# The product with the values placed between the scores of the two tiles of an attention step

## The chip, the cores and the metric

The kernel runs on one core of one Trainium2 chip. The metric is the time of one execution on the device, in microseconds (us); lower is better.

## The reference

Four layers run one after the other over 1024 tokens (4 sequences of 256) of width 512, each with a layer norm ahead of it and a residual behind it: a state-space layer, a sparse feed-forward layer, a latent attention layer, and a clustered feed-forward layer. The change touches the third:

```python
q_c = hidden_size @ Wq_c.T + bq_c
q = (q_c @ Wq_up.T + bq_up).reshape(b, s, NH, Q_HEAD).transpose(0, 2, 1, 3)   # 32 heads, 192 wide
kv = hidden_size @ Wkv_c.T + bkv_c                                            # 64 latent + 64 rope
kvu = (kv_nope @ Wkv_up.T + bkv_up).reshape(b, s, NH, QK_NOPE + V_HEAD)...
scores = jnp.einsum('bhqd,bhkd->bhqk', q, k) / np.sqrt(Q_HEAD)
attn = jax.nn.softmax(scores, axis=-1)
o = jnp.einsum('bhqk,bhkv->bhqv', attn, v)
out = jnp.einsum('bhsv,Hv->bsH', o, Wo) + bo
```

The output projection is the same for every head, so the sum over the heads is formed first. Keys and values are used in their latent form: per head the key weights are folded into the query weights.

## The kernel before

Every engine has its own program, written out by hand, and the engines meet at counting semaphores: `wait_ge` on one side, `then_inc` on the other. What stands in an engine's program runs in that order.

The attention works in tiles numbered `w` from 0 to 127. A tile is one head of one sequence: its 256 queries (two blocks of 128) by 256 keys. `w` counts through 16 head pairs `i`, in each through 4 sequences, in each through the two heads of the pair. The loop of line 1138 takes two tiles in one step, `w` and `w+1`, with `v = w mod 8`, so one pair has four steps: v = 0, 2, 4 and 6. This text calls a step by its `w` or its `v`. On TensorE (PE) a step holds

- `scores(w)` and `scores(w + 1)` (L1054, matmuls L1067 to L1069): 6 matmuls of 128x256 each, since the operands are split into a high and a low part. They write bank `C + w % 2`, so `scores(w)` waits until the exponentials of tile `w - 2` have read that bank (`p_e`);
- in one step of a pair also `fold` (L1011, matmuls L1018) or `fold_bias` (L1027, L1031), which make the folded query weights of the pair after next: for pairs 1 to 13 in the steps v = 2 and v = 4. They stand inside `values`;
- `values` (L1084, matmuls L1100): the product of the probabilities of tiles `w - 4` and `w - 3` with the latent values, into 64-column halves of bank B. It waits for the copied probabilities (`pT`) of tile `w - 3`, and for bank B to be read (`oT`, `oT_l`);
- `turn_p` (L1072, L1080): the transposes of the probabilities of tiles `w - 2` and `w - 1`, which wait for the normalised probabilities (`p_n`);
- `query` (L1034, L1048 to L1052): 5 matmuls of 128x512 for a pair to come, and in the steps v = 0 and v = 4 `sum_up` (L1104, L1108 to L1110), 3 matmuls.

VectorE (DVE) takes one tile after the other (L2066): the row maxima of tile `w` (`top`, L2048 and L2049), then the normalisation of tile `w - 1` (`norm`, L2053 and L2054), and after every second tile the low part of the values' product (L2044) or of a query (L2035). ScalarE (ACT) does in a step (L1627): the exponentials of `w` (`exp`, L1592), what `fold` left (L1560, L1563, L1571), the values' product (`value`, L1608), the copy of the transposes of `w - 2` (L1601), the exponentials of `w + 1`, the copy of the transposes of `w - 1` (L1601 again), and a query (L1584). That last copy of a step is what `values` of the next step waits for: in step `w`, the copy of tile `w - 3`.

Of the kernel before, what the change touches and what calls it, by code (L numbers as in the profile page):

```python
# [37 lines left out]
NV = 2 * NB * NPAIR  # L38
# [5 lines left out]
A, B, C, E, Y0, Y1, T, S = range(8)  # L44
# [20 lines left out]
def bass_layers(nc, d, out):  # L65
    with ExitStack() as ctx:
# [184 lines left out]
        def fold_step(i):  # L251
            return 2 if i else 4
# [8 lines left out]
        def col(n):  # L261
            return slice(n * P, (n + 1) * P)
# [308 lines left out]
        def _(pe):  # L571
# [3 lines left out]
            def busy(n, bank):  # L575

                for _ in range(n):
                    mm(PS[:, bank, 3 * P:], filler[:, 0:P], filler[:, 0:P], start=True, stop=True)  # L578
# [417 lines left out]
            def latent_B(h, bank):  # L996
                for k in range(KD):
                    for n in range(2):
                        last = mm(PS[n * QB:(n + 1) * QB, bank], w_qc[:, k, P:QL], xn[:, k, half(h)], start=(k == 0), stop=(k == KD - 1))
                last.then_inc(s["qc_ps"], 1)  # L1000

            def latent_kv(h, bank):
                project(bank, w_kvc, h).then_inc(s["qc_ps"], 1)

            def keys_turned():
                pe.wait_ge(s["qc"], 6)
                for u in range(NU):
                    last = nc.tensor.transpose(PS[:, S, u * KVL:(u + 1) * KVL], kv[0:KVL, col(u)], identF[0:KVL, 0:KVL])
                last.then_inc(s["qc_ps"], 1)

            def fold(i):  # L1011
                if i:
                    pe.wait_ge(s["cb"], i)
                    pe.wait_ge(s["qb"], i)
                pe.wait_ge(s[f"w_h{i % 2}"], 80 * (i // 2) + 80)
                w = w_h[:, i % 2]
                for n in range(4):
                    last = mm(PS[:, B, SEQ + n * KVL:SEQ + (n + 1) * KVL], w[:, n // 2, col(n % 2)], w[:, n // 2, 2 * P + 1:],  # L1018
                              start=True, stop=True)
                if i < 2:  # L1020
                    fold_bias(i, 0)
                if i == 0:
                    pe.wait_ge(s["a_in"], 16 * 11)
                    mm(PS[KVL:, B, KVL:KVL + NH], bias_rows, identF[0:NH, 0:NH], start=True, stop=True).then_inc(s["qb_ps"], 1)
                last.then_inc(s["cb_ps"], 1)

            def fold_bias(i, at):  # L1027

                w = w_h[:, i % 2]
                for hh in range(2):  # L1030
                    last = mm(PS[0:KVL, B, at + hh:at + hh + 1], w[:, hh, 2 * P + 1:], w[:, hh, 2 * P:2 * P + 1], start=True, stop=True)  # L1031
                last.then_inc(s["qb_ps"], 1)

            def query(i, j):  # L1034
                h, hh = divmod(j, 2)
                pe.wait_ge(s["cb_l"], 2 * i + 2)
                if i == 0 and j == 2:
                    pe.wait_ge(s["ql"], 1)
                elif i == 1 and j == 0:
                    pe.wait_ge(s["ql"], 3)  # L1040
                elif query_bank(i, j) == A and j + i:
                    pe.wait_ge(s["ql"], 4 * i + j)
                R = slice(0, QB)
                a, b, k = 2 * hh, 2 * hh + 1, i % 2
                to = PS[:, query_bank(i, j)]
                if i == 0:
                    pe.wait_ge(s["qc_l"], 3 * h + 2)
                mm(to, lABh[:, k, a], qcAh[:, half(h)], start=True, stop=False)  # L1048
                mm(to, lABh[:, k, a], qcAl[:, half(h)], start=False, stop=False)
                mm(to, lABl[:, k, a], qcAh[:, half(h)], start=False, stop=False)  # L1050
                mm(to, lABh[:, k, b], qcBh[:, half(h)], start=False, stop=False)
                mm(to, lABh[:, k, b], qcBl[:, half(h)], start=False, stop=True).then_inc(s["q_ps"], 1)  # L1052

            def scores(w):  # L1054
                i, v = divmod(w, 2 * NB)
                b, hh = divmod(v, 2)
                pe.wait_ge(s["ql"], 4 * i + b // 2 * 2 + hh + 1)
                if w >= 2:
                    pe.wait_ge(s["p_e"], w - 1)
                elif w == 0:  # L1060
                    pe.wait_ge(s["qc_l"], 3)
                    pe.wait_ge(s["ql"], 2)
                if w == 2 * NB // 2:
                    pe.wait_ge(s["qc_l"], 6)
                for q in range(2):
                    to, c, keys = PS[:, C + w % 2, q * SEQ:(q + 1) * SEQ], col(2 * b + q), slice(b * SEQ, (b + 1) * SEQ)
                    mm(to, qh[i % 2][:, hh, c], kvh[:, keys], start=True, stop=False)  # L1067
                    mm(to, qh[i % 2][:, hh, c], kvl[:, keys], start=False, stop=False)
                    last = mm(to, ql[i % 2][:, hh, c], kvh[:, keys], start=False, stop=True)  # L1069
                last.then_inc(s["s_ps"], 1)  # L1070
# [13 lines left out]
            def values(g, i, v):  # L1084
                b = g % NB
                if g:
                    pe.wait_ge(s["oT"], g)
                    pe.wait_ge(s["oT_l"], g)
                if v == fold_step(i) and i + 2 < NPAIR:
                    fold(i + 2)  # L1090
                elif v == fold_step(i) + 2 and i + 2 < NPAIR:
                    pe.wait_ge(s["cb"], i + 3)
                    fold_bias(i + 2, SEQ)
                else:
                    pe.wait_ge(s["cb"], min(i + 3, NPAIR) if v > 2 else min(i + 2, NPAIR))
                pe.wait_ge(s["pT"], 2 * g + 2)
                pe.wait_ge(s["qc"], 7)
                for kt in range(2):
                    for hh in range(2):
                        last = mm(PS[hh * KVL:(hh + 1) * KVL, B, 0:SEQ], kvT[:, 2 * b + kt], pT[:, (2 * g + hh) % 4, kt],  # L1100
                                  start=(kt == 0), stop=(kt == 1))
                last.then_inc(s["pv_ps"], 1)

            def sum_up(i, h):  # L1104
                k = i % 2
                pe.wait_ge(s["wvl"], i + 1)
                pe.wait_ge(s["oT_l"], NB * i + 2 * h + 2)
                mm(PS[:, Y0 + h], wvh[:, k], oTh[:, half(h)], start=(i == 0), stop=False)  # L1108
                mm(PS[:, Y0 + h], wvl[:, k], oTh[:, half(h)], start=False, stop=False)
                mm(PS[:, Y0 + h], wvh[:, k], oTl[:, half(h)], start=False, stop=(i == NPAIR - 1)).then_inc(s["wv_ps"], 1)  # L1110

            def project_out(h):
                pe.wait_ge(s["bvs"], h + 1)
                if h:
                    pe.wait_ge(s["x3"], KD)
                else:
                    pe.wait_ge(s["pT"], NV - 1)
                for m in range(KD):
                    mm(PS[:, WO_TO[h][m]], w_oT[:, col(m)], osum[:, half(h)], start=True, stop=True).then_inc(s["wo_ps"], 1)  # L1119
# [18 lines left out]
            for w in range(0, NV + 6, 2):  # L1138
                i, v = divmod(w, 2 * NB)
                if w < NV:  # L1140
                    scores(w)
                    scores(w + 1)
                if w == 0:
                    latent_B(1, Y1)
                    latent_kv(1, S)
                if w == 2:
                    keys_turned()
                if NV <= w < NV + 4:
                    busy(20, A)
                if 4 <= w < NV + 4:  # L1150
                    values(w // 2 - 2, i, v)
                if w == NV + 2:
                    busy(24, A)
                    project_out(0)
                if v in (0, 4) and w >= NV:
                    sum_up(i - 1, v // 4)
                if w == 2:
                    query(0, 2)
                    query(0, 3)
                for u in (w, w + 1):  # L1160
                    if 2 <= u < NV + 2:
                        turn_p(u - 2)
                for u in (w, w + 1):
                    if u in QUERY_AT and w > 2:
                        query(*QUERY_AT[u])
                if v in (0, 4) and 2 * NB <= w < NV:
                    sum_up(i - 1, v // 4)
# [1047 lines left out]
```

## Time and profile before

| | |
|---|---|
| median of 3 runs | 2104.95 us (2104.36 to 2105.88) |
| the profiled execution | 2105.0 us, span 2103.2 us |
| TensorE busy | 2066.0 us, 98% |
| VectorE busy | 1603.2 us, 76% |
| ScalarE busy | 1461.1 us, 69% |
| GpSimd busy | 783.9 us, 37% |
| granted TensorE clock | 0.997 of full speed |

Busy time is the union of the records of an engine. The attention loop runs from about 1697 to 2046 us of the span. In rows of the timeline below the first column is the start in us from the span's start, the second the duration in us, then the engine, the line, the operation, its output and input, the shapes and the count; what stands in brackets is idle time of the engine just before, and what ended it.

### The profile page before, as it was taken

How to read it: one execution, taken by the hardware profiler on the slowest of the kernel's cores; microseconds unless marked ns; L12 is line 12 of the kernel's file. 1: busy time of each engine (PE TensorE's matmuls, PEld its weight loads, DVE VectorE, ACT ScalarE, POOL GpSimd, SP SyncE). 2: the span in 40 equal slices, each digit the busy share in tenths (PEclk: the TensorE clock that was granted, in tenths of full speed). 3: DMA queues.
4: the chain of work that ended last, by engine and by line, in shares of the span. 5: the costliest groups of instructions: out<-in, count | busy, mean ns of one | idle time of the engine just before them, and what ended most of it. 6: DMA issues, size and time to landing. Idle time of an engine off the chain costs nothing. (4 is left out here: it accounts for less than half of the span.)

```text
span 2103.2 us, 35260 instructions
## 1 busy us (share of the span) xinstructions
PE 2066.0 (98%) x13530; PEld 1691.3 (80%) x13532; DVE 1603.2 (76%) x1802; ACT 1461.1 (69%) x3188; POOL 783.9 (37%) x433
## 2 busy tenths in 40 slices
PE   8899999999999999999999999999899999999998
PEld 7788888888888888888888888887688768888876
DVE  7778788887877877888788788778653367878775
ACT  4777776777677777677677767775553267787772
POOL 2344444544345444454444543454444300101011
PEclk9999999999999999999999999999999999999999
DMA  3322222222122222222212222122133210101001
GB/s 114 114 81 74 97 101 80 81 101 81 71 101 90 71 101 90 79 92 96 87 71 101 91 71 100 71 99 55 54 98 110 66 46 21 31 21 32 13 2 41
DMA packets 56246, 157.53 MB, mean 75 GB/s; under 512 B 16656, under 2 KB 27152, under 8 KB 47632
## 3 DMA queue, kind: packets, MB, share of 16 engines
q1 hardware_dynamic: 56080, 155.28, 21.4%
q8 instruction: 109, 1.79, 0.3%
q14 instruction: 57, 0.47, 0.1%
HBM read 152.64 MB, written 2.62 MB: 74 GB/s over the span
## 5 line engine op out<-in xcount | busy, mean ns | idle before, releaser
L651 PE MATMUL PS<-xnh,wh 128*128 128x512 f32 x1272 | 510.3, 401 | 3.2 <-DVE arena L1785 1.8
L653 PE MATMUL PS<-xnh,wl 128*128 128x512 f32 x1272 | 496.7, 390 | 0.0
L652 PE MATMUL PS<-xnl,wh 128*128 128x512 f32 x1272 | 495.6, 390 | 0.0
L1779 DVE SCALAR_TENSOR_TENSOR arena<-PS,arena 128x1020 f32<-128x1020 f32 (+2 forms) x240 | 305.6, 1274 | 31.1 <-ACT arena L1328 25.4
L1289 ACT ACTIVATE PS<-x,arena 128x128 f32<-128x128 f32 x1024 | 309.4, 358 | 20.7 <-DVE arena L1811 19.7
L461 POOL TENSOR_TENSOR zl<-arena,zh 128x1024 fp32r<-128x1024 f32 x63 | 176.6, 2803 | 293.7 <-ACT zh L1311 293.7
L651 PEld LDWEIGHTS PS<-xnh,wh 128*128 128x128 f32 x1272 | 238.8, 188 | 57.7 <-issue 8.2
L653 PEld LDWEIGHTS PS<-xnh,wl 128*128 128x128 f32 x1272 | 238.7, 188 | 51.9
L652 PEld LDWEIGHTS PS<-xnl,wh 128*128 128x128 f32 x1272 | 239.3, 188 | 45.7
L457 POOL TENSOR_TENSOR arena<-arena 128x1024 f32<-128x1024 f32 x63 | 151.8, 2409 | 298.0 <-ACT arena L1307 298.0
L446 POOL TENSOR_TENSOR wl<-arena,wh 128x1024 fp32r<-128x1024 f32 x72 | 174.6, 2425 | 198.7 <-ACT wh L1278 198.7
L651 PE MATMUL PS<-zh,woh 128*128 128x512 f32 x496 | 194.2, 392 | 1.4 <-DVE arena L1809 1.4
L653 PE MATMUL PS<-zh,wol 128*128 128x512 f32 x496 | 194.1, 391 | 0.0
L652 PE MATMUL PS<-zl,woh 128*128 128x512 f32 x496 | 193.8, 391 | 0.0
L1817 DVE TENSOR_TENSOR sq<-sq,PS 128x1024 f32<-128x1024 f32 x124 | 150.7, 1221 | 42.9 <-PE PS L653 42.8
L1802 DVE TENSOR_TENSOR arena<-PS,arena 128x1024 f32<-128x1024 f32 x64 | 78.4, 1225 | 130.3 <-PE PS L686 130.3
L710 PE MATMUL PS<-arena 128*64 128x128 f32 x2048 | 171.0, 277 | 4.0 <-DVE arena L1811 4.0
L1324 ACT ACTIVATE arena<-PS 128x1024 f32<-128x1024 f32 x64 | 65.8, 1028 | 147.8 <-PE PS L653 147.8
L1809 DVE TENSOR_TENSOR arena<-PS,arena 128x1024 f32<-128x1024 f32 x128 | 156.1, 1220 | 3.8 <-ACT PS L1293 1.6
L1300 ACT ACTIVATE PS<-x,arena 128x128 f32<-128x128 f32 x512 | 154.5, 360 | 1.5 <-DVE arena L1809 1.5
L1592 ACT ACTIVATE arena<-PS,arena 128x256 f32<-128x256 f32 x256 | 119.4, 474 | 50.7 <-DVE arena L2049 50.4
L710 PEld LDWEIGHTS PS<-arena 128*64 128x64 f32 x2048 | 120.7, 138 | 26.6 <-issue 26.6
(283 smaller groups left out, 4222.6 us busy)
## 6 DMA issues: line engine op xcount, KB each, us to landing
x<-decay SPq DMA_DIRECT2D x64, 1024.0 KB, 4.6
arena<-in_w_xg SPq DMA_DIRECT2D x72, 512.0 KB, 5.4
arena<-in_w_o SPq DMA_DIRECT2D x32, 512.0 KB, 3.5
arena<-in_w_f SPq DMA_DIRECT2D x28, 512.0 KB, 3.5
x<-in_x SPq DMA_DIRECT2D x3, 1024.0 KB, 6.6
arena<-in_w_h SPq DMA_DIRECT2D x16, 192.0 KB, 2.9
arena<-in_w_h SPq DMA_DIRECT2D x16, 129.0 KB, 2.8
out<-x SPq DMA_DIRECT2D x8, 256.0 KB, 2.0
```

The costliest lines, as they stand in the source:

```text
L446: nc.gpsimd.tensor_tensor(wl[:, k], w_raw, wh[:, k].bitcast(F32), ALU.subtract).then_inc(s["wlo"], 1)
L457: nc.gpsimd.tensor_tensor(sumsq, sumsq, ysq, ALU.add).then_inc(s["ssq"], 1)
L461: nc.gpsimd.tensor_tensor(zl[:, k], zt[:, k], zh[:, k].bitcast(F32), ALU.subtract).then_inc(s["zlo"], 1)
L651: mm(PS[:, bank], ah, bh, start=(n == 0), stop=False)
L652: mm(PS[:, bank], ah, bl, start=False, stop=False)
L653: last = mm(PS[:, bank], al, bh, start=False, stop=(n == len(terms) - 1))
L710: last = mm(PS[H, YB + u // 4, col(u % 4)], xdt[:, u, H], ring[:, hh, col(u)], start=(u % 2 == 0), stop=True)
L1289: last = act(PS[:, bank + u // 4, col(u % 4)], rowB[:, 2 * k + hh, col(u)], ACT.Relu, scale=-1.0, bias=aT[:, u, 2 * t + hh:2 * t + hh + 1])
L1300: last = act(PS[:, LB + b // 2, col(2 * hh + b % 2)], rowB[:, 2 * k + hh, col(2 * b + 1)], ACT.Exp, bias=fromend[:, k, b, hh:hh + 1])
L1779: ins = stt(o, pair_of(bank).rearrange("p q (b t) -> p q b t", t=SEQ)[:, :, :, :SEQ - k], w[:, 3 - k:4 - k], o, ALU.mult, ALU.add)
L1809: tt(both(ring[:, hh]), pair_of(bank), both(by[:, 0:TOK]), ALU.mult).then_inc(s["used"], 1)
L1817: tt(both(sq[:, m]), both(sq[:, m]), pair_of(bank), ALU.add).then_inc(s["oacc"], 1)
```

## The change

In the loop over the steps, `values` is written between `scores(w)` and `scores(w + 1)` instead of behind both; what `values` contains (`fold` and `fold_bias` among it) moves with it. Behind the last scores, where a step has none, the order stays as it was. Nothing is added or removed, and the programs of the other engines are untouched.

```diff
                 i, v = divmod(w, 2 * NB)
                 if w < NV:
                     scores(w)
+                elif w < NV + 4:
+                    busy(20, A)
+                if 4 <= w < NV + 4:
+                    values(w // 2 - 2, i, v)
+                if w < NV:
                     scores(w + 1)
                 if w == 0:
                     latent_B(1, Y1)
                     latent_kv(1, S)
                 if w == 2:
                     keys_turned()
-                if NV <= w < NV + 4:
-                    busy(20, A)
-                if 4 <= w < NV + 4:
-                    values(w // 2 - 2, i, v)
                 if w == NV + 2:
                     busy(24, A)
                     project_out(0)
```

TensorE's program in a step v = 6 (`w = 70`), before: from the last matmul of the first tile's scores to the transposes. In brackets stand the semaphores that an instruction waits for.

```order
L1069 MATMUL PS<-xnh,wl 128x256
L1067 MATMUL PS<-xnh,wh 128x256 [waits s_p_e,s_ql]
L1068 MATMUL PS<-xnl,wh 128x256
L1069 MATMUL PS<-xnh,wl 128x256
L1067 MATMUL PS<-xnh,wh 128x256
L1068 MATMUL PS<-xnl,wh 128x256
L1069 MATMUL PS<-xnh,wl 128x256
L1100 MATMUL PS<-arena 64x256 [waits s_pT,s_cb,s_qc,s_oT_l,s_oT]
L1100 MATMUL PS<-arena 64x256 x3
L1080 MATMUL PS<-cst,arena 128x128 [waits s_pT,s_p_n]
L1080 MATMUL PS<-cst,arena 128x128 x3
```

The same stretch now:

```order
L1069 MATMUL PS<-xnh,wl 128x256
L1100 MATMUL PS<-arena 64x256 [waits s_pT,s_cb,s_qc,s_oT_l,s_oT]
L1100 MATMUL PS<-arena 64x256 x3
L1067 MATMUL PS<-xnh,wh 128x256 [waits s_p_e,s_ql]
L1068 MATMUL PS<-xnl,wh 128x256
L1069 MATMUL PS<-xnh,wl 128x256
L1067 MATMUL PS<-xnh,wh 128x256
L1068 MATMUL PS<-xnl,wh 128x256
L1069 MATMUL PS<-xnh,wl 128x256
L1080 MATMUL PS<-cst,arena 128x128 [waits s_pT,s_p_n]
L1080 MATMUL PS<-cst,arena 128x128 x3
```

The four matmuls of `values`, with their five waits, have moved ahead of the six of the second tile's scores; the transposes stay where they were. The steps v = 0 have the same rows.

TensorE's program in a step v = 4 of a pair with a fold (`w = 76`), now: from the last matmul of the first tile's scores.

```order
L1069 MATMUL PS<-xnh,wl 128x256
L1031 MATMUL PS<-arena 64x1 [waits s_cb,s_oT_l,s_oT]
L1031 MATMUL PS<-arena 64x1
L1100 MATMUL PS<-arena 64x256 [waits s_qc,s_pT]
L1100 MATMUL PS<-arena 64x256 x3
L1067 MATMUL PS<-xnh,wh 128x256 [waits s_p_e,s_ql]
L1068 MATMUL PS<-xnl,wh 128x256
L1069 MATMUL PS<-xnh,wl 128x256
L1067 MATMUL PS<-xnh,wh 128x256
L1068 MATMUL PS<-xnl,wh 128x256
L1069 MATMUL PS<-xnh,wl 128x256
```

Before, the last six of these rows stood ahead of the first L1031.

## Rows read from the trace of the kernel before

**Rows 1.** Windows view, one head pair: busy us and records by engine, clock, DMA

```profile
1889.90:1911.14 21.24, 21.22 (x152) 17.47 (x150) 17.01 (x40) 16.91 (x53) 2.23 (x3) 1.00 0.10 26
```

**Rows 2.** Timeline of PE, step w = 72 (v = 0)

```profile
1894.55 0.28 PE L1067 MATMUL PS<-xnh,wh 128*128 128x256 f32 x1
...
1895.87 0.28 PE L1069 MATMUL PS<-xnh,wl 128*128 128x256 f32 x1
1896.08 1.09 PE L1100 MATMUL PS<-arena 128*64 128x256 f32 x8
1897.10 1.09 PE L1080 MATMUL PS<-cst,arena 128*128 128x128 f32 x8
...
1899.88 0.28 PE L1067 MATMUL PS<-xnh,wh 128*128 128x256 f32 x1
```

**Rows 3.** Timeline of PE, step w = 76 (v = 4)

```profile
1905.35 0.28 PE L1067 MATMUL PS<-xnh,wh 128*128 128x256 f32 x1
...
1905.94 0.28 PE L1069 MATMUL PS<-xnh,wl 128*128 128x256 f32 x1
1906.24 0.35 PE L1067 MATMUL PS<-xnh,wh 128*128 128x256 f32 x1
1906.44 0.28 PE L1068 MATMUL PS<-xnl,wh 128*128 128x256 f32 x1
```

**Rows 4.** Timeline of ACT, at the same place

```profile
1905.53 0.49 ACT L1592 ACTIVATE arena<-PS,arena 128x256 f32<-128x256 f32 x1
1905.88 0.22 ACT L1592 ACTIVATION_READ_ACCUMULATOR arena<-PS,arena 128x1 f32 x1
1905.97 0.62 ACT L1601 ACTIVATE arena<-PS 128x512 f32<-128x512 f32 x1
```

**Rows 5.** Line L1067: idle time of its engine (us, times) by what ended it

```profile
  issue: 4.1, 16
```

**Rows 6.** Timeline of DVE and ACT, end of step w = 70 (v = 6)

```profile
1893.09 0.68 DVE L2048 TENSOR_REDUCE arena<-PS 128x2 f32<-128x512 f32 x1
1894.01 0.48 ACT L1592 ACTIVATE arena<-PS,arena 128x256 f32<-128x256 f32 x1 [0.27 <-DVE arena L2049]
1894.93 0.59 ACT L1601 ACTIVATE arena<-PS 128x512 f32<-128x512 f32 x1
```

**Rows 7.** Timeline of ACT and PE behind the last scores: copy, then values

```profile
2039.47 0.61 ACT L1601 ACTIVATE arena<-PS 128x512 f32<-128x512 f32 x1
2040.33 1.09 PE L1100 MATMUL PS<-arena 128*64 128x256 f32 x8 [0.74 <-ACT arena L1601]
```

**Rows 8.** Timeline of PE and ACT, step w = 120, last of its kind

```profile
2020.65 0.28 PE L1067 MATMUL PS<-xnh,wh 128*128 128x256 f32 x1
2021.04 0.60 ACT L1601 ACTIVATE arena<-PS 128x512 f32<-128x512 f32 x1
```

**Rows 9.** Timeline of PE, ACT and DVE, fold step w = 74 (v = 2)

```profile
1900.80 0.69 DVE L2048 TENSOR_REDUCE arena<-PS 128x2 f32<-128x512 f32 x1 [1.05 <-PE PS L1069]
1902.25 1.09 PE L1100 MATMUL PS<-arena 128*64 128x256 f32 x8
1903.07 0.68 DVE L2048 TENSOR_REDUCE arena<-PS 128x2 f32<-128x512 f32 x1
1903.38 0.38 ACT L1560 ACTIVATE arena<-PS 128x256 f32<-128x256 f32 x1 [0.63 <-PE PS L1100]
1904.60 0.59 ACT L1601 ACTIVATE arena<-PS 128x512 f32<-128x512 f32 x1
```

**Rows 10.** Timeline of PE and ACT, step w = 124

```profile
2030.05 0.28 PE L1069 MATMUL PS<-xnh,wl 128*128 128x256 f32 x1
2031.25 0.36 PE L1067 MATMUL PS<-xnh,wh 128*128 128x256 f32 x1 [0.92 <-ACT arena L1592]
2032.13 1.09 PE L1100 MATMUL PS<-arena 128*64 128x256 f32 x8
2031.00 0.60 ACT L1601 ACTIVATE arena<-PS 128x512 f32<-128x512 f32 x1
```

## The prediction

> **What bounds the kernel now.** The change touches the attention loop alone, so I read that stretch. The windows view of one head pair comes first: in 21.24 us TensorE is busy 21.22, VectorE 17.01, ScalarE 16.91 [rows 1], at full granted clock. The loop is bound by TensorE, and only two things can move its time: idle time in TensorE's queue, and extra cost where one kind of matmul follows another. The busy share cannot show a short wait, because the record of a scores matmul lasts 0.28 us while the next one starts 0.12 us later (1905.35 to 1905.94 are five such distances [rows 3]). So I read distances between starts, in the timeline.
>
> Nearly every distance is regular. The six matmuls of one tile's scores take 6 x 0.12 = 0.72 us, from the last scores to the values it is 0.21, from the values to the transposes 1.02 [rows 2]. One exception recurs. In step v = 4 of a pair the second tile's scores start 0.30 us after the matmul before them and the next follows after 0.20, where 0.12 is normal: 0.18 + 0.08 = 0.26 us lost [rows 3]. ScalarE shows why: the exponentials of tile w-1, which read the same bank, end at 1905.88 + 0.22 = 1906.10, and the scores start 0.14 us later [rows 4]. It happens in pairs 1 to 13, the ones whose fold delays ScalarE; the summary of line L1067 has 4.1 us of such idle time in 16 places [rows 5], which includes a few at the loop's ends. A second exception is step w = 124, where the second scores start 1.20 us after the matmul before them, again for the exponentials [rows 10]. Almost nothing else on TensorE is waiting, so there is little to gain: 13 x 0.26 = 3.4 us, and about 1.1 us in w = 124.
>
> The Trainium skill (Perfetto Trace Analysis, section Tensor Engine Instruction) says that the end of a matmul in the profile is an estimate from its size. By busy time alone, 0.02 us idle in a pair, the gain would be 13 x 0.02 = 0.3 us in place of 3.4; the starts are recorded, and I go by them.
>
> **The change part by part.** No instruction is added or removed, no DMA moves. 62 steps (w = 4 to 126) have both scores and values and change their order. Each part is the change in TensorE's time, which in a TensorE-bound loop is the change of the kernel.
>
> *The wait that goes.* In step v = 4 about 1.2 us of work (the fold's bias and the values) now lies ahead of the second scores. They come 0.72 + 1.2 = 1.9 us after 1905.35 [rows 3], long after 1906.10. Gain 13 x 0.26 = 3.4 us.
>
> *The wait that comes.* The values need the copied probabilities of tile w-3, which is the last copy ScalarE makes in the step before. In step w = 72 that copy ends at 1894.93 + 0.59 = 1895.52, 0.97 us after the step's first scores at 1894.55 [rows 2, 6]. The values used to start 1.53 us after them (1896.08), now they would after 1.53 - 0.72 = 0.81. So the copy is late. How long after it the values can start is shown behind the last scores, where TensorE stands idle for exactly this: copy ends 2039.47 + 0.61 = 2040.08, values start 2040.33, 0.25 us later [rows 7]. The values then start at 0.97 + 0.25 = 1.22, a stall of 0.41 us. TensorE works in order, so the second scores and all behind them stand still too.
>
> Can the copy come earlier? It follows the exponentials of tile w-1, which start when VectorE has their maxima: 1893.09 to 1894.01, with ScalarE idle for 0.27 us just before [rows 6]. VectorE in turn is full from the first scores of step v = 6 on, taking a tile each 2.3 us, and that start is not moved relative to its step. So the copy stays where it is relative to TensorE, and earlier values do not help it. The stall should appear wherever the step before is a short one, 4.65 us as from 1889.90 to 1894.55 [rows 1, 2]: the 15 steps v = 0 (w = 8 to 120, where the last has the copy's end at 2021.04 + 0.60 = 2021.64, 0.99 us after the scores at 2020.65 [rows 8]), and w = 116, whose step before has no fold. Behind longer steps, with a sum or a fold, the copy ends at 0.3 us or before the scores: no stall.
>
> *The fold steps.* Three things shift in step v = 2. The values come 0.72 us earlier, so ScalarE's 0.63 us wait for them goes [rows 9] and its chain runs ahead. The values start at 1902.25 - 0.72 = 1901.53, the second scores at 1902.55, and the row maxima 0.92 us behind them (1899.88 to 1900.80 for the first tile [rows 2, 9]), at about 1903.5 in place of 1903.07. The exponentials follow another 0.92 later [rows 6], at 1904.4, unless the copy ahead of them holds them: it starts at 1904.60 now [rows 9] and about 0.55 sooner then, since the transposes stay where they are and let it come no earlier. So exponentials and last copy move up 0.5 to 0.6 us, and that copy ends near 1906.59 - 0.6 = 1906.0 [rows 4], 0.65 us after the first scores of step v = 4. With 0.25 added that is 0.90, just ahead of the values there at about 1.0. I cost this at nothing. The cover is thin: if it is gone, step v = 4 has the 0.41 stall too.
>
> *The order of matmul kinds.* The values are 64 columns wide, all around them 128. A step had scores, values, transposes; it now has scores, values, scores, transposes. The number of width changes is the same. New is that scores restart behind the values. When scores restart after a pause, the first takes 0.20 us to the next where 0.12 is normal [rows 3]: 0.08. The transposes no longer restart after the values and give back up to that much. Ends: nothing and 0.08 us a step. I take 0.03, nearer the low end because one restart replaces another: 62 x 0.03 = 1.9 us. In the 16 steps with a stall, that 0.03 of the step before shortens the stall to 0.38: 16 x 0.38 = 6.1 us.
>
> The Trainium skill (TensorEngine Tiling (Array Packing), section Key Properties) says that changing the tiling mode drains TensorE. By that rule alone, both orders have two such changes in a step and this term is zero; the whole sum would be 1.9 us lower. No row here has values followed by scores, so the row of the restart decides.
>
> *The end of the loop.* Without queries the steps are short and TensorE is ahead of ScalarE. In w = 124 the copy that the values need ends at 2031.00 + 0.60 = 2031.60; the values start at 2031.85 (before: 2032.13) and the second scores 1.02 later at 2032.87 (before: 2031.25) [rows 10]. The transposes follow about 0.5 us later than now. In w = 126 the same repeats, with the last scores some 2 us and the last tile's exponentials some 0.9 us later than now; nothing behind them takes up the delay. Cost 0.9 us, ends 0 and 1.5.
>
> Sum: -3.4 + 6.1 + 1.9 + 0.9 = +5.5 us. The profiled execution took 2105.0 us, the median of the runs is 2104.95, so the two hardly differ: 2105.0 + 5.5 = 2110.5 us.
>
> **The rivals.**
> *The new wait is cheap.* The 0.25 us from copy to values is measured on an engine that had stood idle; with 0.6 us of scores running it may partly hide, and the copy may shift. With 0.15 in place of 0.38: -3.4 + 2.4 + 1.9 + 0.5 = +1.4, 2106.4 us, within the noise. For it: only 0.97 against 0.81 is bare lateness. Against: the stretch from copy to values is passing on a signal, which running scores don't shorten.
>
> *Faster.* ScalarE's last copy of a step moves up. If it ends less than 0.81 - 0.25 = 0.56 us after the first scores everywhere, no values wait, the 3.4 us come in whole, and the 1.2 us hole of w = 124 is filled: 2105.0 - 3.4 - 1.2 = 2100.4 us. For it: ScalarE loses the wait for the values in the fold steps. Against: in step v = 6 it waits for VectorE, not for TensorE [rows 6], and that end must come 0.4 us sooner.
>
> *Slower than forecast.* The fold steps' second scores come so late that VectorE and ScalarE carry the delay into step v = 4: values there stall 0.38 us as well, in 13 pairs. 5.5 + 13 x 0.38 = +10.4, 2115.4 us. It decides at a copy that ends later than 0.75 us after the first scores of step v = 4, against my 0.65.
>
> That the change doesn't do what it says can be ruled out: the program's order shows the rows moved.
>
> **How the numbers follow.** About 0.2% (4.2 us) is what a measurement of this kernel can tell from no change. Chances: forecast 0.53, cheap wait 0.25, slower than forecast 0.14, faster 0.08. The forecast's own ends, from a restart at nothing (-1.9, tail -0.9) to one at 0.08 (+3.1), are 2107.7 and 2113.6; a quarter of it lies below 2109.2 and counts as no change. The cheap wait is almost wholly within 0.2%. So slower 0.55, same 0.37, faster 0.08. The range takes in the forecast, the cheap wait with a free restart (2104.5) and nearly all of the slower case: 2104 to 2115.
>
> **What would show each step right or wrong.** In the profile after: the copy still ends 0.97 us after the first scores in steps v = 0, values start 1.22 after them, and TensorE is idle there; a pair takes 21.24 - 0.26 + 0.38 + 0.12 = 21.48 us. In step v = 4 the second scores wait for nothing. ScalarE's wait for the values in fold steps is gone. The distance from a first score behind the values to the next is near 0.20, and from the last scores to the transposes 0.12. The forecast is wrong if values in steps v = 0 start before 1.0, if steps v = 2, 4 or 6 show a wait of the values, or if a pair takes 21.24 us or less.

## The result and the profile after

The changed kernel takes 2110.77 us (median of 8 runs, 2109.33 to 2111.98), the kernel before 2104.51 us beside it (8 runs, 2102.06 to 2107.66). The ratio is 1.0033 with a 95% interval of 1.0023 to 1.0042: slower by 6.3 us, where 5.5 us and a time of 2110.5 us had been forecast.

Single executions of one kernel differ by up to some 3 us from the median, and much of that arises ahead of the attention: in the traces of this study its first matmul (L999) starts anywhere between 1679.2 and 1683.5 us. So the traces are compared by two lengths that leave this out. One is a head pair, from the first scores of w = 70 to those of w = 78. The other is the attention stretch, from the first matmul of `latent_B` (L999) to the first of the output projection (L1119). The summaries of these two lines in the trace of the changed kernel (durations in ns, then first and last start in us):

```profile
L999 PE MATMUL PS<-arena x32: 592/592/643, 1680.2 to 1699.5; 128*64 128x512 f32 x32
```

```profile
L1119 PE MATMUL PS<-arena x16: 591/592/697, 2051.3 to 2060.9; 128*128 128x512 f32 x16
```

The stretch is 371.13 us by the timeline's hundredths. In the kernel before it was 364.55 (1682.42 to 2046.97). The whole difference of 6.58 us is there; what lies behind it takes 56.25 us in both.

The windows view of the changed kernel, the same head pair as in [rows 1] (columns as there: length; busy us and records of PE, weight loads, VectorE, ScalarE, GpSimd; granted clock, DMA share, GB/s):

```profile
1889.39:1910.90 21.51, 21.20 (x152) 17.65 (x150) 17.08 (x40) 16.82 (x54) 2.23 (x3) 1.00 0.10 25
```

21.51 against 21.24 us: the pair is 0.27 us longer, and TensorE's busy time has not grown. The time went into waits. The timeline of TensorE in step w = 72 (v = 0), which answers to [rows 2]:

```profile
1894.06 0.28 PE L1067 MATMUL PS<-xnh,wh 128*128 128x256 f32 x1
...
1894.66 0.28 PE L1069 MATMUL PS<-xnh,wl 128*128 128x256 f32 x1
1895.25 1.09 PE L1100 MATMUL PS<-arena 128*64 128x256 f32 x8 [0.31 <-ACT arena L1602]
1896.26 0.39 PE L1067 MATMUL PS<-xnh,wh 128*128 128x256 f32 x1
1896.49 0.28 PE L1068 MATMUL PS<-xnl,wh 128*128 128x256 f32 x1
...
1896.96 0.28 PE L1069 MATMUL PS<-xnh,wl 128*128 128x256 f32 x1
1897.09 1.03 PE L1080 MATMUL PS<-cst,arena 128*128 128x128 f32 x8
...
1899.81 0.28 PE L1067 MATMUL PS<-xnh,wh 128*128 128x256 f32 x1
```

And ScalarE's copy that it waited for:

```profile
1894.40 0.60 ACT L1602 ACTIVATE arena<-PS 128x512 f32<-128x512 f32 x1
```

The copy ends at 1895.00, 0.94 us after the first scores, and the values start 0.25 us behind it, 1.19 us after those scores instead of the 0.80 us that they take in steps without a wait. The step is 5.75 us long (before: 5.33). The view of waits from 1715 to 2040 us (who waited for whom: us, times, longest) has it as a line of its own, which the kernel before did not have in this window:

```profile
PE PS L1100 <- ACT arena L1602: 6.7, 17, 1.5
```

The 17 places are 14 of the steps v = 0 and the steps w = 116, 124 and 126. The fifteenth step v = 0, w = 8, is not among them: its copy ends at 0.71 and its values start at 0.96, so it loses only 0.16 us to the wait.

Steps v = 4 of the pairs with a fold have lost their wait. TensorE in step w = 76, which answers to [rows 3]:

```profile
1905.31 0.28 PE L1067 MATMUL PS<-xnh,wh 128*128 128x256 f32 x1
...
1905.91 0.28 PE L1069 MATMUL PS<-xnh,wl 128*128 128x256 f32 x1
1906.12 0.34 PE L1031 MATMUL PS<-arena 128*64 128x1 f32 x3
...
1907.36 0.38 PE L1067 MATMUL PS<-xnh,wh 128*128 128x256 f32 x1
1907.58 0.28 PE L1068 MATMUL PS<-xnl,wh 128*128 128x256 f32 x1
```

Everything follows at the normal distances. The step takes 5.58 us (before: 5.79). Its copy, on ScalarE:

```profile
1905.33 0.60 ACT L1602 ACTIVATE arena<-PS 128x512 f32<-128x512 f32 x1
```

It ends 0.62 us after the first scores, and the values start normally at 0.95. Steps v = 2 with a fold take 5.50 us (before 5.47), steps v = 6 take 4.67 (before 4.65). So a pair changes by +0.41 - 0.21 + 0.03 + 0.02 = +0.25, and 0.27 in the windows.

Added up over the loop, step by step: 14 steps v = 0 at +0.415 and w = 8 at +0.18 make +6.0; w = 116 +0.4; 13 steps v = 4 -2.7; 13 steps v = 2 +0.4; 13 steps v = 6 +0.3; w = 6, which had a wait of its own, -0.2; the other steps up to w = 122 +0.2; w = 124 +0.4; and from the first scores of w = 126 to the output projection +1.7 (13.94 against 12.20). That is +6.5. The last item was not foreseen in this size. VectorE there, between the last scores and the last values but one, in the changed kernel:

```profile
2041.45 1.02 DVE L2050 TENSOR_SCALAR arena<-arena 128x2 f32<-128x2 f32 x1
2042.39 0.15 DVE L2054 RECIPROCAL arena<-arena 128x2 f32<-128x2 f32 x1
2042.57 1.64 DVE L2055 TENSOR_TENSOR arena<-arena 128x512 f32<-128x512 f32 x1
2044.14 0.41 DVE L2045 TENSOR_TENSOR xnl<-PS,xnh 128x256 fp32r<-128x256 f32 x1
2044.47 0.15 DVE L2054 RECIPROCAL arena<-arena 128x2 f32<-128x2 f32 x1
2044.66 1.24 DVE L2055 TENSOR_TENSOR arena<-arena 128x512 f32<-128x512 f32 x1
```

These operations elsewhere take 0.17 (L2050) and 0.69 us (L2055). At the same time GpSimd works on the next layer's weights, and TensorE waits for VectorE's low part:

```profile
2041.19 5.85 POOL L560 TENSOR_TENSOR zl<-arena,zh 128x512 fp32r<-128x512 f32 x4
```

```profile
2044.65 1.09 PE L1100 MATMUL PS<-arena 128*64 128x256 f32 x8 [1.98 <-DVE xnl L2045]
```

### The profile page after: what moved, and what is told of

Its sections match the earlier page's. It is cut to its first block, busy times and chain, and to the rows that moved or that the text cites. A ratio compares the mean times of both kernels' runs of the same rounds, so it can differ in the third digit from the quotient of the medians.

```text
span 2107.6 us, 35262 instructions
## 1 busy us (share of the span) xinstructions
PE 2064.1 (98%) x13532; PEld 1692.6 (80%) x13532; DVE 1605.1 (76%) x1802; ACT 1457.3 (69%) x3188; POOL 784.2 (37%) x433
## 4 chain that ended last, share of the span: by engine, by line
PE 87%; DVE 7%; ACT 2%; issue 1%; DMA 1%; SPq 1%; POOL 0%; ACTq 0%; DVEq 0%
PE PS L651 19%; PE PS L653 19%; PE PS L652 19%; PE PS L710 6%; PE PS L919 3%; PE PS L686 3%; PE PS L706 3%; PE PS L1100 2%; PE PS L1080 2%; PE PS L1067 1%; DVE arena L2049 1%; PE PS L1069 1%; PE PS L1068 1%; DVE arena L1780 1%; PE PS L644 1%
```

## The experiments

Two theories stood against each other. **The waits**: the change costs where the values wait for ScalarE's copy, in the steps behind a short step and at the loop's end, and gains where the scores no longer wait for the exponentials. **The restart**: scores behind values cost some 0.10 us in each of the 62 steps. Both give the 6.6 us, but at different places. Runs 1, 2, 3 and 5 choose the order step by step. They use this form of the loop, each with a condition of its own (the edit is against the changed kernel):

```diff
+                between = 4 <= w < NV and (CONDITION)
                 if w < NV:
                     scores(w)
                 elif w < NV + 4:
                     busy(20, A)
-                if 4 <= w < NV + 4:
+                if between:
                     values(w // 2 - 2, i, v)
                 if w < NV:
                     scores(w + 1)
+                if 4 <= w < NV + 4 and not between:
+                    values(w // 2 - 2, i, v)
```

| kernel | attention stretch, us | against before | time, us (ratio to before, 95%) |
|---|---|---|---|
| before | 364.55 | | |
| the change | 371.13 | +6.58 | 2110.77 (1.0033, 1.0023 to 1.0042) |
| 1: v = 4 alone | 364.70 | +0.15 | 2104.83 (1.0005, 0.9997 to 1.0014) |
| 2: v = 0 alone | 370.98 | +6.43 | 2110.01 (1.0030, 1.0019 to 1.0040) |
| 3: old order in w = 124, 126 | 368.75 | +4.20 | 2108.61 (1.0023, 1.0015 to 1.0032) |
| 4: change, GpSimd late | 369.87 | +5.32 | 2108.46 (1.0023, 1.0014 to 1.0032) |
| 5: v = 2 and v = 4 | 362.13 | -2.42 | 2101.42 (0.9988, 0.9979 to 0.9997) |
| 6: change, copy's wait first | 368.95 | +4.40 | 2109.31 (1.0023, 1.0014 to 1.0032) |
| 7: change, slower copy | 377.08 | +12.53 | 2115.26 (one execution) |
| 8: before, slower copy | 364.49 | -0.06 | 2106.02 (one execution) |
| 9: before, GpSimd late | 364.57 | +0.02 | 2102.11 (one execution) |
| 10: as 5, GpSimd late | 361.99 | -2.56 | 2099.4 (one execution) |

**1. The new order in the fold steps v = 4 alone** (CONDITION: `v == 4 and i + 2 < NPAIR`). The condition takes in w = 4 of the first pair too, so 14 steps change.

> The values go between the scores only in the 13 steps v = 4 whose pair folds; the other 49 steps keep the order of before. Theory of the waits (what the change costs hangs on where it is made): these steps lose their wait for the exponentials and are 0.20 us shorter each, no values wait for a copy; 13 x 0.20 = 2.6 us faster than before, a head pair takes 21.24 - 0.20 = 21.04 us. Theory of the restart (scores behind values cost some 0.10 us in each place, 6.6 us over 62 steps): 13 x 0.10 = 1.3 us slower than before.

Nothing came: the stretch is 0.15 us longer, and the 13 fold steps take 5.82 or 5.83 us, 0.04 more than before and not the 5.58 expected. Step w = 6 behind w = 4 is 0.24 us shorter, which takes back about half of that. This falls under neither theory as I had put it. The timeline of TensorE and ScalarE in step w = 76, whose first scores start at 1904.66:

```profile
1905.25 0.28 PE L1069 MATMUL PS<-xnh,wl 128*128 128x256 f32 x1
1905.46 0.39 PE L1031 MATMUL PS<-arena 128*64 128x1 f32 x4
1905.95 1.09 PE L1100 MATMUL PS<-arena 128*64 128x256 f32 x8
```

```profile
1905.28 0.62 ACT L1605 ACTIVATE arena<-PS 128x512 f32<-128x512 f32 x1
```

The copy ends at 1905.90, 1.24 us after the first scores as in the kernel before, and the values wait for it in place of the scores. In the changed kernel it ends at 0.62, because there the values of step v = 2 are moved as well and let ScalarE's `fold` start sooner; run 5, which moves both, has it at 0.62 again. The gain of one step hangs on the order of the step before. The run gave one more thing: here the values start 0.05 us behind the copy, not 0.25.

**2. The new order in the 15 steps v = 0 alone** (CONDITION: `v == 0`).

> The values go between the scores only in the 15 steps v = 0. Theory of the waits: the values wait for the copy there and each step is 0.41 us longer (the first of them 0.2): 15 steps make 5.9 us over before, nearly the whole of the loss, a head pair takes 21.24 + 0.41 = 21.65 us, and no step v = 4 gains. Theory of the restart: 15 x 0.10 = 1.5 us over before.

The stretch is 6.43 us longer, the 15 steps take 5.76 to 5.78 us and the pair 21.67:

```profile
1890.16:1911.83 21.67, 21.30 (x152) 17.57 (x150) 17.09 (x40) 16.80 (x53) 2.22 (x3) 1.00 0.11 26
```

15 of 62 places carry almost the whole loss. The restart theory, which gave 1.5 us, falls.

**3. The old order in the last two steps** (CONDITION: `w < NV - 4`).

> As the change, but the steps w = 124 and 126 keep the order of before. Theory of the waits: the last two steps and what follows them cost 2.2 us in the changed kernel (0.44 in step 124, 1.73 behind the first scores of step 126), and with the old order there this goes: 6.6 - 2.2 = 4.4 us over before. Theory of the restart: 60 of the 62 places are left, 6.4 us over before.

+4.20 us against 4.4 expected: the end of the loop is worth 2.4 us, with 12.19 us from the first scores of w = 126 to the output projection, as before.

**4. GpSimd's next work held back.**

```diff
+            po.wait_ge(s["p_n"], NV)
             for k in range(KD):
                 po.wait_ge(s["wd_h"], k + 1)
```

> The changed kernel, with GpSimd's four subtractions for the next layer's weights (L560) waiting for the last normalisation. Theory of the collision (those 5.9 us of GpSimd work slow VectorE's last tiles: L2050 took 1.02 instead of 0.17 us, L2055 1.64 and 1.24 instead of 0.69): these durations return to normal and the kernel is 1.5 to 2 us faster than the changed one, some 4.8 us over before. If the two only happen at the same time, the durations stay and the time is that of the changed kernel.

VectorE's durations returned to normal, where the changed kernel had 1.02 and 1.64:

```profile
2040.58 0.17 DVE L2051 TENSOR_SCALAR arena<-arena 128x2 f32<-128x2 f32 x1
2040.65 0.16 DVE L2055 RECIPROCAL arena<-arena 128x2 f32<-128x2 f32 x1
2040.84 0.69 DVE L2056 TENSOR_TENSOR arena<-arena 128x512 f32<-128x512 f32 x1
```

So the subtractions do slow them. The gain in the stretch is 1.26 us, a little under the 1.5 to 2 us expected: once VectorE is on time, ScalarE's copy is the next wait.

**5. The new order in the steps v = 2 and v = 4 of pairs 1 to 13** (CONDITION: `v in (2, 4) and 0 < i and i + 2 < NPAIR`).

> The values go between the scores in the steps v = 2 and v = 4 of the 13 pairs 1 to 13, and nowhere else. The first run with v = 4 alone kept ScalarE's late copy (1.24 us after the first scores), because the values of step v = 2 were not moved. Theory of the waits, mended: with both moved the copy of step v = 2 ends 0.6 us after the first scores of step v = 4 as in the changed kernel, steps v = 4 take 5.58 us (before 5.79) and steps v = 2 take 5.50 (before 5.47), the others stay: a pair takes 21.24 - 0.17 = 21.07 us, 2.3 us less over the loop. Theory of the restart: 26 restarts and no wait gone, 2.6 us more.

All of it came. The steps take 5.58 (v = 4) and 5.50 us (v = 2), the others keep their lengths, the stretch is 2.42 us shorter than before, and the pair:

```profile
1886.29:1907.36 21.07, 21.07 (x152) 17.51 (x150) 17.02 (x40) 16.89 (x54) 2.23 (x3) 1.00 0.11 27
```

By the distances between starts, no step of this pair has a wait left on TensorE. The time is 2101.42 us against 2104.43 beside it, ratio 0.9988 with an interval that ends below 1. This version is faster than both kernels.

**6. The copy's wait written first.** In steps without a fold:

```diff
+                plain = i + 2 >= NPAIR or v not in (fold_step(i), fold_step(i) + 2)
+                if plain:
+                    pe.wait_ge(s["pT"], 2 * g + 2)
                 if g:
                     pe.wait_ge(s["oT"], g)
...
-                pe.wait_ge(s["pT"], 2 * g + 2)
+                if not plain:
+                    pe.wait_ge(s["pT"], 2 * g + 2)
```

> The changed kernel, with the wait for the copied probabilities written first of the five waits of the values, so that it is the one taken last in front of the matmul. Theory of the queued waits (0.20 of the 0.25 us from copy to values are the other waits, taken one after the other behind it; in the run with v = 4 alone, where that wait stood alone with one other, the values started 0.05 us behind the copy): in steps v = 0 the values start 1.00 us after the first scores instead of 1.19, each such step takes 5.55 instead of 5.75 us, and with w = 116, 124 and 126 some 3.5 us go. Rival (0.25 us is the price of the signal from ScalarE to an idle TensorE): nothing changes.

Half of it came. The timeline of ScalarE, VectorE and TensorE in step w = 72, whose first scores start at 1895.14:

```profile
1895.48 0.59 ACT L1606 ACTIVATE arena<-PS 128x512 f32<-128x512 f32 x1
```

```profile
1895.61 0.41 DVE L2049 TENSOR_TENSOR xnl<-PS,xnh 128x256 fp32r<-128x256 f32 x1
```

```profile
1896.23 0.44 PE L1104 MATMUL PS<-arena 128*64 128x256 f32 x2 [0.21 <-ACT arena L1606]
```

The values start 1.09 us after the first scores instead of 1.19, 0.16 us behind the copy's end at 1896.07. Thirteen of the steps v = 0 (w = 16 to 112) take 5.63 instead of 5.75 us, and the stretch is 2.18 us shorter than in the change. What held these steps can be read from the trace; the bracket names ScalarE because its signal came last, but TensorE was not yet at that wait. TensorE takes the five waits in three places, one behind the other: two of them, two more, and the last at the load of the weights. Here the first place holds the wait for VectorE's low part (`oT_l`), and the trace has it as an entry of its own (`source` view of that line from 1894.5 to 1896.1 us; duration in ns, start in us):

```profile
L1098 PEldq EVENT_SEMAPHORE  x1: 2042/2042/2042, 1894.0 to 1894.0; - x1
```

It begins at 1894.02 and ends at 1896.07, 0.05 us behind the low part's end at 1896.02. The second place is entered at 1896.12, and at 1896.20 the load of the weights, which has the wait for the copy, starts: the copy had ended by then. So in these steps it is the low part that has waits queued behind it, 0.21 us from its end to the values. In steps where the low part is early, nothing of this is left. ScalarE and TensorE in step w = 120 of the same run:

```profile
2022.50 0.28 PE L1067 MATMUL PS<-xnh,wh 128*128 128x256 f32 x1
2022.86 0.60 ACT L1606 ACTIVATE arena<-PS 128x512 f32<-128x512 f32 x1
2023.51 1.09 PE L1104 MATMUL PS<-arena 128*64 128x256 f32 x8
```

The low part ended 0.42 us ahead of this copy. The values start 0.05 us behind the copy and 1.01 us after the first scores, where the expectation had 1.00; the step takes 5.54 us, where it had 5.55. Steps w = 116 and 124 show the same 0.05. In the changed kernel these three steps have 0.25 like the others: there the copy's wait stands in the first place, the second is entered at 1895.14 in step w = 72 and the load starts at 1895.22. So 0.20 of the 0.25 us are the other waits queued behind the copy's, as expected, and the rival is wrong. In the steps v = 0 of the change the low part ended only 0.06 us ahead of the copy (1894.94 against 1895.00), which is why it takes over so soon here.

**7 and 8. A slower copy.** A dummy operation on ScalarE ahead of the last copy of steps v = 6, in the change and in the kernel before (it computes nothing that is used):

```diff
+                if v == 6 and w < NV - 8:
+                    act(spare, cst[:, 0:SEQ], ACT.Copy)
                 if 2 <= w < NV + 2:
                     copy(w - 1)
```

> The changed kernel with a dummy copy of 128x256 on ScalarE ahead of the last copy of the steps v = 6 (w = 6 to 118, 15 times). Theory of the waits: the values in steps v = 0 wait for ScalarE's copy, so each such step grows by what the dummy adds to ScalarE's chain, 0.26 to 0.30 us: 6.02 us instead of 5.75, 4 us in all. If the step's length is set by VectorE's low part of the product or by the restart of the matmuls, it stays at 5.75.

> The kernel before with the same dummy copy. The copy ends then at about 0.97 + 0.28 = 1.25 us after the first scores of steps v = 0, and with 0.25 more that is 1.50, just ahead of the values at 1.53. Theory of the waits: steps v = 0 stay at 5.33 us and the time stays within 0.5 us. If ScalarE's work itself were the bound, the loop would grow by 4 us here as in the changed kernel.

In the change the copy ends 1.24 us after the first scores instead of 0.94, the values start at 1.49 instead of 1.19, and the steps v = 0 take 6.05 us instead of 5.75: the 0.30 us on the copy are 0.30 us on the step. VectorE's low part did not move, so it is the copy that ends this wait. TensorE in step w = 72, first scores at 1896.30:

```profile
1897.79 1.09 PE L1101 MATMUL PS<-arena 128*64 128x256 f32 x8 [0.62 <-ACT arena L1603]
```

In the kernel before, the same 0.3 us cost nothing. Its copy ends at 1.27 and its values start at 1.53 as ever, the pair stays at 21.22 us:

```profile
1896.31 0.59 ACT L1602 ACTIVATE arena<-PS 128x512 f32<-128x512 f32 x1
```

```profile
1897.16 0.44 PE L1101 MATMUL PS<-arena 128*64 128x256 f32 x2
```

The old order gave ScalarE a slack of 0.3 us there; the new one takes the slack and 0.4 us more. The seventh run's stretch grew by 5.95 us over the change, not by 4: 4.4 us in the steps up to w = 126, and 1.57 at the end, from something else. There TensorE stood idle for 1.98 us as in the change, and from 0.3 us behind the idle time on the granted clock was 0.50, the lower level of 1.2 GHz. The windows view:

```profile
2049.30:2052.70 3.40, 3.40 (x14) 2.11 (x11) 1.35 (x2) 0.38 (x1) 2.06 (x2) 0.50 0.02 5
```

The values there take 1.73 us instead of 1.09. In the changed kernel's profile the clock stayed at 1.00 at this place.

**9 and 10. GpSimd late in the kernel before, and in the version of run 5** (the edit of run 4).

> The kernel before, with GpSimd's four subtractions (L560) waiting for the last normalisation. Theory of the collision as a matter of order: the two last normalisations (L2054, 0.94 and 1.07 us) return to 0.69, but nothing on the path waits for them, since the values behind the last scores wait for ScalarE's copy: the stretch from the first scores of w = 126 to the output projection stays at 12.2 us within 0.1. If the collision cost the kernel before as well, that stretch gets 0.5 us or more shorter.

> The version with the values between the scores in the steps v = 2 and v = 4 alone, with the same late subtractions. Its last steps are those of before, so the stretch from the first scores of w = 126 to the output projection stays at 12.2 us too, and the loop at 362.1 us.

From w = 126 to the output projection both take 12.2 us, as before. The stretch is 364.57 in the one, 361.99 in the other (run 5: 362.13). The collision with GpSimd's subtractions is there in the kernel before too: its last L2054 takes 1.07 us, and 0.69 in run 9. The one ahead of it takes 0.94 us and still 0.93 in run 9, against the expectation; another GpSimd operation (L540, 0.45 us) runs beside it in both. By the trace nothing on the path waited for either. The collision came onto the path through the change.

## Why the prediction was right, point by point

- *What bounds the kernel.* Right. The lengths of the steps changed by what TensorE waits for, and by 0.02 to 0.05 us a step for the new order of its matmuls; runs 7 and 8 show that ScalarE's work as such costs nothing until TensorE waits for it.
- *The wait that goes.* Forecast -3.4 us. The wait went in all 13 steps. They became 0.21 us shorter each, -2.7 us, which includes a restart; the forecast had both, 13 x (0.26 - 0.03) = 3.0, so the restart is 0.05 us in these steps. What the working did not say is that this gain needs the moved values of step v = 2 as well: run 1 shows that without them all of it is lost to the values' own wait.
- *The wait that comes.* Forecast at 16 places, 1.22 us after the first scores, +6.1 us. It is at those 16, at 1.19 in all but two (0.96 in the first, w = 8, which loses only 0.18 us, and 1.28 in w = 32); the copy ends 0.94 instead of 0.97 us after the first scores. It makes +6.4 with the steps' restarts in it, where the forecast had 16 x 0.41 = 6.6. Run 2 and the pair of runs 7 and 8 show that this wait, and ScalarE's copy as what ends it, is the cost. The 0.25 us from copy to values, read behind the last scores, held exactly, because the same waits stand in the same order there. The prediction's reason for it was wrong: it called the time the passing on of a signal, and run 6 shows that 0.20 us of it is the queue of the other waits and 0.05 what is left where the copy's wait is the last.
- *The fold steps.* The copy was put at 0.65 us after the first scores of step v = 4 and came at 0.62; no wait of the values there, as costed. The rival that this cover fails did not come true in the change, but is what run 1 shows.
- *The order of matmul kinds.* Forecast 0.03 us a step. In steps where nothing waits it is 0.02 (v = 6) to 0.03 us (v = 2), in the steps with the copy's wait 0.03 as well (0.41 longer, 0.39 of it the wait), and in the fold steps v = 4 0.05; that is about 2 us in all against 1.9. The scores behind the values take 0.22 us to the next matmul, and the transposes follow the scores at the normal distance, as expected. The rule of the Trainium skill on mode changes (TensorEngine Tiling (Array Packing), Key Properties), which with two changes in either order gives zero, is nearly right too: the rest is 0.02 to 0.05 us a step, but over 62 steps that is the 2 us.
- *The end of the loop.* The step that was mis-sized: 0.9 us forecast, with ends 0 and 1.5; the trace has 0.4 in w = 124 and 1.7 behind, 2.2 us, and run 3 gives back 2.4. I followed the dependences of the last tile, but with VectorE's durations from the middle of the loop. They grew to 1.02, 1.64 and 1.24 us from 0.17, 0.69 and 0.69, because the last tile had moved under GpSimd's subtractions; run 4 gives 1.26 us of it back. The remaining 1 us is what was forecast.
- *The rivals.* The cheap wait fails: running scores hide nothing of the 0.25 us. The faster case needed a copy that ends 0.56 us after the first scores in steps v = 0; it ends at 0.94. The slower case needed one later than 0.75 in steps v = 4; it ends at 0.62. The head pair takes 21.51 us, where the forecast gave 21.48. Of the 6.6 us measured, 1.1 were not forecast: the end of the loop came out 1.3 above its term, the fold steps v = 4 0.3 above, and the rest together some 0.5 below.

## What to carry to other kernels

Filling a wait of one engine with other work moves that work's own waits forward: before moving a group, take the latest arrival of each of its inputs relative to the new start, in every kind of step, and add the time from signal to start that an idle engine shows elsewhere in the trace, from a place where the same waits stand in the same order. Where several waits stand ahead of one instruction, the one that is met last should be the one that is taken last, as in run 6. A loop whose steps differ can want a different order in each: here the order pays in the two fold steps together, pays nothing in v = 4 alone (v = 2 alone was not run), and costs in the steps v = 0, 0.41 us each, and a little in the rest. And a chain that is delayed at the end of a loop may land beside the next stage's work on another engine; its durations must be taken from there.

## What the runs showed of the hardware

- The distance from the end of the last input to the first matmul depends on how many waits stand behind that input's: 0.25 us with the copy's wait among the first of five (the change), 0.05 with it last of five (run 6, w = 116, 120 and 124) and 0.05 where the other waits were on an earlier matmul (run 1). In the change TensorE reaches the second place of waits 0.11 us after the first, and the load with the last wait 0.08 us after that.
- GpSimd subtractions of 128x512 running beside VectorE stretched a VectorE operation on 128x2 elements from 0.17 to 1.02 us and two on 128x512 from 0.69 to 1.64 and 1.24 (run 4 against the change).
- After 1.98 us of idle time TensorE's granted clock stayed at 1.00 in the profile of the change, and fell to 0.50 (1.2 of 2.4 GHz) from 2049.3 to 2052.7 us in run 7, which cost 1.57 us. In run 6 the idle time at the same place is 2.28 us and the clock stayed at 1.00. What decided is open.
